# Eight heads a step in the two narrow attentions of a four-layer transformer kernel

## The reference, cut to what matters

```python
# layer 0, plain
scores = einsum('bthd,bshd->bhts', wq, wk) / sqrt(8)
probs = softmax(scores, axis=-1)
attn = einsum('bhts,bshd->bthd', probs, wv)
# layer 2, pruned: as above, and between the two products
col_sum = sum(probs, axis=2)                 # over the queries, for each key
_, idx = top_k(col_sum, int(128 * 0.9))      # keep 115 of 128 keys a head
probs = probs * mask(idx)[:, :, None, :]
```

## Time and profile before

| | us |
|---|---|
| median of 3 runs | 988.65 (988.4 to 996.85) |
| profiled execution, first to last instruction | 983.6 |
| first (plain) narrow attention, first score product to last copy | 20.3 to 112.05 |
| second (pruned) narrow attention, the same | 628.1 to 742.05 |
| PE busy over the span | 842.0 (86%) |
| DVE, ACT, POOL busy | 532.1, 363.7, 328.1 |

### The profile page before, as it was taken

The page is one execution under the profiler, slowest core; times in us unless marked ns, Lnnn a source line. Parts: engine busy times, 40 slices in busy tenths (PEclk is TensorE's granted clock), DMA queues, the critical chain, the costliest instruction groups (busy, mean ns, idle before and its releaser), DMA issues. The chain is left out here.

```text
span 983.6 us, 18321 instructions
## 1 busy us (share of the span) xinstructions
PE 842.0 (86%) x5450; PEld 717.9 (73%) x5450; DVE 532.1 (54%) x1605; ACT 363.7 (37%) x1158; POOL 328.1 (33%) x321
## 2 busy tenths in 40 slices
PE   4999689998799999986489997699976899999556
PEld 2666478998599999984369997455545789989555
DVE  5466675444666666655643334566664544444554
ACT  1466232443154545442123443366641422221202
POOL 4577421220344343420221221566525224220100
PEclk9699869999999999997779999755555999999577
DMA  3000000113000000000001112000001020110000
GB/s 146 2 1 0 22 12 24 41 43 129 5 2 2 1 0 1 0 0 1 6 27 33 43 43 69 1 1 0 0 1 55 1 65 33 32 53 11 0 1 22
DMA packets 11474, 22.80 MB, mean 23 GB/s; under 512 B 1416, under 2 KB 5536, under 8 KB 11168
## 3 DMA queue, kind: packets, MB, share of 16 engines
q1 hardware_dynamic: 11424, 22.20, 6.8%
HBM read 21.67 MB, written 0.52 MB: 23 GB/s over the span
## 5 line engine op out<-in xcount | busy, mean ns | idle before, releaser
L752 PEld LDWEIGHTS bank<-weights_out,hidden 128*128 128x128 f32 x1664 | 197.2, 194 | 9.2 <-issue 4.5
L752 PE MATMUL bank<-weights_out,hidden 128*128 128x128 f32 x1664 | 198.2, 277 | 4.2 <-PEq L1011 4.2
L703 ACT ACTIVATE hidden<-bank,cols 128x512 f32<-128x512 f32 x144 | 98.0, 688 | 147.4 <-ACTq L701 147.3
L1556 DVE SCALAR_TENSOR_TENSOR x_tok<-bank,combine_weights,x_tok 128x128 f32<-128x128 f32 x256 | 72.3, 345 | 141.0 <-DVEq L1537 140.8
L548 POOL TENSOR_SCALAR weights_in_hi<-weights_in 128x256 fp32r<-128x256 f32 (+2 forms) x34 | 52.5, 1545 | 247.7 <-POOLq L547 247.7
L752 PE MATMUL bank<-input_hi,weights_in_lo 128*128 128x512 f32 x280 | 120.4, 430 | 12.9 <-PEq L982 7.5
L639 ACT ACTIVATE probabilities<-bank,neg_max 128x128 f32<-128x128 f32 x256 | 90.4, 365 | 65.0 <-ACTq L636 65.0
L752 PE MATMUL bank<-input_lo,weights_in_hi 128*128 128x512 f32 x280 | 114.1, 408 | 0.0
L752 PE MATMUL bank<-input_hi,weights_in_hi 128*128 128x512 f32 x280 | 113.5, 405 | 0.0
L487 POOL TENSOR_TENSOR rstd<-var_eps,neg_half 128x4 f32<-128x4 f32 x24 | 25.1, 1048 | 210.9 <-POOLq L486 196.1
L527 POOL TENSOR_TENSOR probabilities<-probabilities,inverse_sums 128x512 f32<-128x512 f32 x64 | 66.2, 1040 | 43.8 <-POOLq L525 17.3
(11 more groups left out here) (195 smaller groups left out, 1511.4 us busy)
## 6 DMA issues: line engine op xcount, KB each, us to landing
weights_out<-w_in SPq DMA_DIRECT2D x17, 256.0 KB, 2.7
weights_in<-w_in SPq DMA_DIRECT2D x8, 512.0 KB, 3.9
weights_in<-w_in SPq DMA_DIRECT2D x9, 256.0 KB, 2.9
weights_in<-w_in SPq DMA_DIRECT2D x16, 128.0 KB, 2.2
weights_out<-w_in SPq DMA_DIRECT2D x16, 128.0 KB, 2.0
wq<-w1q_in SPq DMA_DIRECT2D x1, 1024.0 KB, 5.0
wo<-w1o_in SPq DMA_DIRECT2D x1, 1024.0 KB, 7.1
rows<-rows_in SPq DMA_DIRECT2D x1, 976.5 KB, 6.7
```

The costliest lines, as they stand in the source:

```text
L703: act.activation(hT[:, half, fc, :], bank[f.hidden_bank(n, fc)][:, :], f.first, **kw)\
L752: return pe.matmul(o, l, rh, start=start, stop=stop, **kw)
L1556: dve.scalar_tensor_tensor(x[:, b, :], ps[:, t, :], cw[:, b, bass.ds(e, 1)], x[:, b, :], ALU.mult, ALU.add).then_inc(st.sem, st.one())
```

## The change

The unit of a step becomes eight heads: half a batch. The plain attention has 4 steps a loop turn (two batches), the pruned one 8 steps (four batches, two loop turns in all). PSUM is allotted as four pairs of banks; scores use pairs 0 and 1, the transposes pair 2 alone, outputs pair 3.

- `scores` issues its three kinds of product alternately for two row groups, into two banks.
- `maxima`, `inverse_sums`, the copies out of the transposes, `column_sums` and `normalise` handle eight heads an instruction; `exps` stays one instruction per head.
- Plain: `normalise` on POOL is gone. The inverse sums are written eight times over (`inverse_sums_wide`), transposed on PE once a batch, and multiply the output (`scale_out`: a copy and a product, 128x128 each). `values` runs once a batch over four column groups.
- Pruned: the ranking, its two transposes, `keep_values` and `copy_out` run once for two batches, on 32 partitions, so half as often. A second buffer for the turned probabilities lies in the tile `hidden`.
- The lags change with it: `turn`, its copies and `column_sums` now all have lag 2.

Core of the diff, DVE and PE:

```diff
 # DVE
                 def maxima(it, n):
-                    if n % 4 == 3:
+                    if n % 2 == 1:
                         dve.sem_inc(qk_free, 1)
-                    dve.tensor_reduce(neg_max[:, n, :], b4(n % 2), X_AX, ALU.max, negate=True)\
+                    dve.tensor_reduce(neg_max8[:, n % 4, :], b8(n % 2), X_AX, ALU.max, negate=True)\
                         .then_inc(neg_max_ready, 1)
...
+                def scale_out(it, n):
+                    dve.wait_ge(out_done, 1)
+                    dve.sem_inc(out_done, -1)
+                    dve.sem_inc(v_free, 1)
+                    at = n // 2
+                    dve.tensor_copy(out_copy[:, at, :], bank[6 + at][:, 0:P]).then_inc(st.sem, st.one())
+                    dve.wait_ge(st.sem, st.n)
+                    dve.tensor_tensor(attT[:, bass.ds((2 * it + at) * P, P)], out_copy[:, at, :],
+                                      bank[6 + at][:, 256:256 + P], ALU.mult).then_inc(st.sem, st.one())
...
                 if prune:
-                    order = [(maxima, range(8), 0), (inverse_sums, range(8), 1), (rank, (3, 7), 5),
-                             (keep_values, (3, 7), 6), (column_sums, range(8), 4), (copy_out, (3, 7), 8)]
+                    pipelined(dve, [(maxima, range(8), 0), (inverse_sums, range(8), 1), (rank, (3, 7), 3),
+                                    (keep_values, (3, 7), 4), (copy_out, (3, 7), 6),
+                                    (column_sums, range(8), 2)], 8, NB // 4, st.close)
                 else:
-                    order = [(maxima, range(8), 0), (inverse_sums, range(8), 1), (copy_out, (3, 7), 5),
-                             (copy_probsT, range(8), 3)]
+                    pipelined(dve, [(maxima, range(4), 0), (inverse_sums, range(4), 1), (scale_out, (1, 3), 4),
+                                    (copy_probsT, range(4), 2)], 4, NB // 2, st.close)
 # PE
                 def scores(it, n):
...
-                    split_products(bank[n % 2][:, :],
...
+                    for left, right in ((q_b_lo, k_mask_hi), (q_b_hi, k_mask_lo), (q_b_hi, k_mask_hi)):
+                        for g in range(2):
+                            p = slice(32 * (2 * (n % 2) + g), 32 * (2 * (n % 2) + g) + 32)
+                            m = mm(bank[2 * (n % 2) + g][:, :], left[p, at, :],
...
                 if prune:
-                    pipelined(pe, [(scores, range(8), 0), (turn, range(8), 3), (turn_sums, (3, 7), 5),
-                                   (turn_kept, (3, 7), 6), (values_kept, (3, 7), 7)], 8, NB // 2,
+                    pipelined(pe, [(scores, range(8), 0), (turn_sums, (3, 7), 3), (turn_kept, (3, 7), 4),
+                                   (values_kept, (3, 7), 5), (turn, range(8), 2)], 8, NB // 4, lambda: None)
                 else:
-                    pipelined(pe, [(scores, range(8), 0), (turn, range(8), 3), (values, range(8), 4)],
+                    pipelined(pe, [(scores, range(4), 0), (values, (1, 3), 3), (turn, range(4), 2)],
+                              4, NB // 2, lambda: None)
 # ACT, pruned
-                    pipelined(act, [(exps, range(8), 0), (copy_probsT, range(8), 2)], 8, NB // 2, st.close)
+                    pipelined(act, [(exps, range(8), 0), (copy_probsT, range(8), 2)], 8, NB // 4, st.close)
 # POOL
-                pipelined(pool, [(spread_queries_keys, (0, 4), 0), (spread_values, (0, 4), 5),
-                                 (normalise, range(8), 5)], 8, NB // 2, st.close)
+                if prune:
+                    pipelined(pool, [(spread_queries_keys, (0, 2, 4, 6), 0), (normalise, range(8), 2),
+                                     (spread_values, (0, 2, 4, 6), 4)], 8, NB // 4, st.close)
+                else:
+                    pipelined(pool, [(spread_queries_keys, (0, 2), 0), (spread_values, (0, 2), 3)],
+                              4, NB // 2, st.close)
```

More of the change, by code:

```diff
@@ L182, in build @@
         col_sum = sb("column_sums", [P, 2, H])
-        ranked = sb("ranked", [H, P + 8])
-        top = sb("top", [H, 2, 8])
-        kept = sb("kept", [H, P])
+        ranked = sb("ranked", [2 * H, P + 8])
+        top = sb("top", [2 * H, 2, 8])
+        kept = sb("kept", [2 * H, P])
         logits = sb("logits", [P, NB, E1])
@@ L219, in w, with b8 @@
             return sq[:, at + i:at + i + (n or size)]
-        bank = [ctx.enter_context(nc.psum_tensor(f"bank{i}", [P, 512], F32)) for i in range(8)]
+        banks = [ctx.enter_context(nc.psum_tensor(f"banks{i}", [P, 2, 512], F32)) for i in range(4)]
+        bank = [banks[i // 2][:, i % 2, :] for i in range(8)]
         def b4(i):
             return bank[i][:, :].rearrange("p (a b) -> p a b", a=4)
+        def b8(i):
+            return banks[i][:, :, :].rearrange("p c (a b) -> p (c a) b", a=4)
         x_loaded = sem("x_loaded")
@@ L636, in exps @@
                     act.sem_inc(neg_max_ready, -1)
-                    for i in range(4):
-                        h = 4 * (n % 4) + i
-                        act.activation(prob[:, n // 4, h, :], b4(n % 2)[:, i, :], ACT.Exp,
-                                       bias=neg_max[:, n, i:i + 1], accum_out=z[:, n // 4, h:h + 1])\
-                            .then_inc(st.sem, st.one())
+                    for i in range(8):
+                        h = 8 * (n % 2) + i
+                        act.activation(prob[:, n // 2 % 2, h, :], b8(n % 2)[:, i, :], ACT.Exp,
+                                       bias=neg_max8[:, n % 4, i:i + 1],
+                                       accum_out=z[:, n // 2 % 2, h:h + 1]).then_inc(st.sem, st.one())
                     act.wait_ge(st.sem, st.n)
@@ L644, in exps @@
                     act.sem_inc(exps_done, 1)
+                    if not prune:
+                        act.sem_inc(probs_ready, 1)
                 def copy_probsT(it, n):
@@ L657, in narrow_attention @@
                 if prune:
-                    pipelined(act, [(exps, range(8), 0), (copy_probsT, range(8), 2)], 8, NB // 2, st.close)
+                    pipelined(act, [(exps, range(8), 0), (copy_probsT, range(8), 2)], 8, NB // 4, st.close)
                 else:
-                    pipelined(act, [(exps, range(8), 0)], 8, NB // 2, st.close)
+                    pipelined(act, [(exps, range(4), 0)], 4, NB // 2, st.close)
             def wide_attention():
@@ L802, in turn, with head_outputs @@
                     pe.sem_inc(turn_free, -1)
+                    for i in range(8):
+                        t = pe.transpose(b8(2)[:, i, :], prob[:, n // 2 % 2, 8 * (n % 2) + i, :], ident[:, :])
+                    t.then_inc(probsT_done, 1)
+                def head_outputs(o, source, turned, at):
                     for i in range(4):
-                        t = pe.transpose(b4(2 + n % 2)[:, i, :], prob[:, n // 4, 4 * (n % 4) + i, :],
-                                         ident[:, :])
@@ L806, in turn @@
-                    t.then_inc(probsT_done, 1)
-                def head_outputs(source, parity, groups):
-                    for i in range(4):
-                        for j in groups:
+                        for j in range(4):
                             h = 4 * j + i
-                            m = mm(bank[6 + parity][32 * j:32 * j + 32, 0:P], source[:, parity, h, :],
-                                   probT[:, parity, h, :], start=(i == 0), stop=(i == 3))
+                            m = mm(o[32 * j:32 * j + 32, :], source[:, at, h, :], turned[:, at, h, :],
+                                   start=(i == 0), stop=(i == 3))
@@ L1258, in inverse_sums @@
                     dve.sem_inc(exps_done, -1)
-                    h = slice(4 * (n % 4), 4 * (n % 4) + 4)
-                    dve.reciprocal(r[:, n // 4, h], z[:, n // 4, h]).then_inc(st.sem, st.one())
+                    h = slice(8 * (n % 2), 8 * (n % 2) + 8)
+                    at = n // 2 % 2
+                    if prune:
+                        dve.reciprocal(r[:, at, h], z[:, at, h]).then_inc(st.sem, st.one())
+                    else:
+                        dve.reciprocal(r_wide[:, at, h, :], z[:, at, h][:, :, None].broadcast_to([P, 8, DH]))\
+                            .then_inc(st.sem, st.one())
                     dve.wait_ge(st.sem, st.n)
@@ L1275, in copy_out @@
                     dve.sem_inc(out_done, -1)
-                    if not prune:
-                        dve.sem_inc(v_free, 1)
-                    dve.tensor_copy(attT[:, bass.ds((2 * it + n // 4) * P, P)], bank[6 + n // 4][:, 0:P])\
+                    dve.tensor_copy(attT[:, bass.ds((4 * it + n // 2 - 1) * P, 2 * P)], bank[6][:, 0:2 * P])\
                         .then_inc(st.sem, st.one())
```

126 lines of the change are left out of this document (70 added, 56 removed).

## The result

The changed kernel takes **999.5 us** (12 runs, 997.3 to 1000.6), the kernel before on the same chip 990.9 (12 runs, 987.0 to 997.0): a ratio of **1.0084, 95% interval 1.0059 to 1.0109**. In four later measurements the kernel before had medians of 988.2 to 988.8. Forecast were 983 and 970 to 992; it came out 0.8% slower, outside the range.

What follows compares the result with a forecast made beforehand. PE was taken to bound the plain attention, ACT and DVE's ranking the pruned one. Terms -6.3 and +0.7 sum to -5.6 on the profiled 983.6, thus 978.0, or 983 us in the runs against 988.65; range 970 to 992.

Steps and rivals of the forecast that it cites:

- Both rings: Waits in a circle between engines: 6.48 us a step in the pruned attention; 9.3 (full clock) or 10.3 (low) a batch in the plain.
- the two signs: The forecast is wrong if pruned exponential groups come every 4.5 us, or if PE is full.
- the pruned term: Pruned attention: 12.96 us a batch against 12.98, end at 742.7 against 742.05, so +0.7 us.
- the copy to the column sum: Pruned attention, ACT's copy to DVE's column sum: 0.86 us, with ends 0.43 (term -5) and 1.2 (term +5).
- the tail: Pruned attention, from the start of the last exponentials at 721.2 to the end: 21.5 us.
- rival C: Pruned attention: the circle of waits does not close, ACT alone bounds with 4.5 a step; -26, kernel 957; chance 0.08.
- The plain term: Plain attention: end at 102.3 or 109.3 us by clock, middle 105.8, against 112.05, so -6.3 us.
- That the clock would change between its levels: Plain attention: PE busy 6.5 of 9.3 at full clock, 10.1 of 10.3 at low; clock alternates, middle taken.
- The values at full clock: Plain attention: value products take 1.93 us at full clock, as at the low one; 0.96 would give 8.3 a batch.
- rival A: Plain attention: clock goes up and values take half, 8.3 us a batch; -14, kernel 974; chance 0.20.
- Rival B: Score products in two row groups do not overlap on PE: 12.4 us a plain batch at low clock; kernel 1001; chance 0.07.
- The ranking: Pruned attention, DVE: 2.35 us, done half as often; saves time only where none is lost any more.

Runs made afterwards that it cites:

- Taking the ring away: Column sums, and the stages behind them, one step later in the pruned attention, against the changed kernel: 972.8 us, 26.8 under it.
- PE kept busy and the wait last: 18 unread transposes a batch ahead of PE's wait for the second-half copy, plain attention, against the changed kernel with that wait moved last (995.5): 985.2 us.

## Why the prediction was wrong

Its forecast was -5.6: +0.7 and -6.3. Measured are +9.7 and +1.3 by stretches, and +0.65 behind the plain attention. Both rings were where it put them, and neither of the two signs that it had named for being wrong appeared: the exponential groups did not come every 4.5, and PE was not full. Terms in the sums of the rings were wrong.

1. **The failed step of the pruned term is the copy to the column sum, put at 0.86 and measured at 1.37.** The ring, its place and its four links were right; the three others were met within 0.02. The 0.86 was twice the 0.43 between the copy at 644.33 and the column sum at 644.76 in the earlier trace rows. But these two don't wait for each other. Two more rows of before show it:

```profile
641.63 0.60 ACT L650 ACTIVATE probabilities_keys<-bank 128x512 f32<-128x512 f32 x1 [0.27 <-ACTq L648]
...
644.32 0.18 DVE L1260 RECIPROCAL inverse_sums<-exp_sums 128x4 f32<-128x4 f32 x1 [0.32 <-DVEq L1258]
```

Counted from the loop's start, 644.76 is the third column sum and 641.63 the third copy, which had ended 2.5 us earlier. The column sum began where it did because DVE's reciprocal had ended at 644.50; the 0.43 was a coincidence of two engines, not a hand-over. The real one is the whole copy, 1.02, plus 0.35, and the upper end of 1.2 was too low as well, since it left the hand-over out. With 0.52 more a ring, and 0.14 of waits ahead of the maxima, thirteen rings took 92.8 us instead of 84.2; the tail took 22.7 instead of 21.5. These 8.6 and 1.2 and the forecast 0.7 make 10.5, and the two profiled executions differ by 10.4. Taking the ring away gave 26.8 us, which rival C had as 26. That is partly luck: C went from steps of 6.48 to 4.5, the runs from 7.1 to 5.0, and what opened the ring was an edit of the order and not an earlier copy.

2. **The plain term failed on its hand-over, the reciprocal and the clock.** The ring of second-half copy, values, turn, copy, maxima, reciprocal and copy out is as described. Copy to values was put at 0.15 behind the copy's end and took 0.65, because of the order of four waits. The reciprocal to the copy out was put at 0.6 and took 0.89, since it writes 64 columns. That the clock would change between its levels was forecast, but the mean of a full-clock ring and a low-clock ring (9.8) is not what alternating gave: the clock was up where PE mostly waited, and down for the turn behind the values, which is on the ring. Measured rings were 10.2 to 11.0. In the two executions compared, the stretch fell from 107.0 to 105.9, by 1.2 where 6.3 was forecast. Seven rings, from second-half copy to second-half copy, took 72.0 where 7 x 9.8 less 1.2 was put, 67.4: that is 4.6 of the 5.1 missed. The other 2.5 up to the mean of +1.3 are the spread of both codes' executions. That the attention ended at 109.3, the very end that the prediction had for the low clock alone, is luck: the clock was not low throughout, and the rings were longer than its 10.3 in part.

3. **The values at full clock** were put at 1.93 and take 1.01 from their start to the next instruction's, in rings with the clock held up. The Trainium skill (TensorE: Matmul & The Clock Gate, section "Wait — 56ns, not 53.3ns?") gives some 62 ns a matmul with hardware decode off, which gives an estimate of 1.98 for 32. The trace has 32 records in 1.01, 32 ns each, so that bound was not in force here; no run shows whether decode was on or off, and the page's figure is neither confirmed nor refuted. The measurement decides, and rival A was right on the values. Its ring of 8.3 is near the 8.6 measured with PE kept busy and the wait last. It failed on its condition, that the clock stays up by itself.

4. **Rival B** did not happen: six score products in two row groups take what three take. With eight heads, the next instruction starts 1.58 us after the first score product at the low clock and 0.90 at the full one; with four heads it was 1.58 and 0.89.

5. **What one execution could not show.** The profiled execution of before had a plain stretch of 107.0, where its four executions range over 6 us with a mean of 105.9. In every run with both numbers the span lies 1.7 to 2.1 us under the execution's own time; so that execution was one of about 985.3, some 3 under the median, and not a median one read 5.05 too low. A term of a few us in a stretch that varies like this cannot be read against one execution.

6. **The ranking.** It is half as often, as described, and it did not matter, because DVE has 1.3 to 4.5 us idle ahead of each column sum, 1.3 of them left in the steps with a ranking. What it is worth with the ring open was not tried by itself.

## What to carry to other kernels

When a lag shrinks so that a stage consumes what is produced in the same step, write down the ring and price each hand-over as the producer's whole duration plus the time from its end to the consumer's start, from a place in the trace where the consumer really waited for that producer; a short distance between two instructions that don't wait for each other is no price. Put the wait that is satisfied last behind the others. Work taken off PE is not all gain: here PE's idle time went with a low clock for the next products on the ring, and 144 useless transposes that filled it held the clock at 1.00 and were worth 10.3 us.

## What the runs showed of the hardware

- Three waits that had long been satisfied, each with its decrement, took 0.46 us behind the one that ended last (0.65 against 0.19). Two posts ahead of the one that mattered took 0.15 (copy to column sum 1.37 against 1.22).
- 32 records of products with 32 columns, spread over four column groups, take 1.94 us at the low clock and 1.08 at the full one; the next instruction starts after 1.86 and 1.01.
- A reciprocal that writes 64 columns, reading each of 8 sums eight times, takes DVE 0.54 us, of 8 columns 0.20: some 6 ns for each further column. From 512 to 1024 columns a maxima goes from 0.69 to 1.22, 1.0 ns each.
- The same program has 58 or 36 matmul records in the same 10 us, by the moment at which the clock rises, and its executions lie up to 13.6 us apart in one measurement.
